# Norm affine parts on GpSimd, the shared expert last, and `dbu` four states at a time, in a Mamba plus mixture-of-experts layer

## What is computed

```python
xn = layernorm(x)
x_proj, z = split(xn @ W_in + b_in)             # 256 + 256 channels
u  = silu(x_proj)
B, C = split(u @ W_xproj + b_xproj)             # 16 states each
dt = softplus(u @ W_dt + b_dt)
h_t = h_(t-1) * exp(dt_t * A) + (dt_t * u_t) * B_t      # per channel and state
y_t = sum over states of h_t * C_t, + D * u_t
x = x + (y * silu(z)) @ W_out + b_out
xn2 = layernorm(x)
scores = softmax(xn2 @ gate_w.T); top 2 of 8 by scores + gate_bias
x = x + sum_e mlp(xn2, w1[e], w2[e], w3[e]) * weight_e + mlp(xn2, sw1, sw2, sw3)
mlp(x, w1, w2, w3) = (silu(x @ w1.T) * (x @ w3.T)) @ w2.T
```

## Time and profile before

| | |
|---|---|
| median of three runs | 1247.91 us |
| the profiled execution's own time | 1250.07 us |
| its span in the trace | 1248.3 us |
| PE busy | 1167.9 us (94%) |
| DVE busy | 1140.5 us (91%) |
| ACT busy | 1140.1 us (91%) |
| POOL (GpSimd) busy | 1043.5 us (84%) |
| DMA, mean | 122 GB/s |

### The profile page before, as it was taken

One profiled execution on the slowest core, in us unless ns is written; L12 is line 12 of the kernel. 1 busy time (PEld: TensorE's weight loads), 2 busy tenths in 40 slices (PEclk: granted clock), 3 DMA queues, 4 the chain that ended last, 5 costly groups with the idle time before them and its releaser, 6 DMA issues.

```text
span 1248.3 us, 24503 instructions
## 1 busy us (share of the span) xinstructions
PE 1167.9 (94%) x7200; PEld 952.1 (76%) x7200; DVE 1140.5 (91%) x1833; ACT 1140.1 (91%) x1980; POOL 1043.5 (84%) x534
## 2 busy tenths in 40 slices
PE   6465699999999999999999999999999999999998
PEld 2244487878888787887878788888878788888887
DVE  0799999999999999999999999999999999999853
ACT  5674989999999999999999999999999999998854
POOL 2998999998998898999889899899889989986500
PEclk8666899999999999999999999999999999999999
DMA  7434150703325060433406042331506133150000
GB/s 265 181 128 153 39 242 9 288 11 146 152 83 207 9 274 23 156 140 136 160 13 275 8 192 104 145 151 62 225 8 250 46 145 143 71 219 1 18 10 9
DMA packets 47955, 152.91 MB, mean 122 GB/s; under 512 B 4512, under 2 KB 29472, under 8 KB 31392
## 3 DMA queue, kind: packets, MB, share of 16 engines
q1 hardware_dynamic: 47904, 152.28, 31.8%
HBM read 147.03 MB, written 5.24 MB: 122 GB/s over the span
## 4 chain that ended last, share of the span: by engine, by line
POOL 44%; PE 23%; issue 18%; ACT 9%; DVE 3%; DMA 1%; POOLq 1%; ACTq 0%; DVEq 0%; SPq 0%
POOL dbu L767 31%; PE h L1034 10%; POOL hc L777 8%; PE mixed L1003 6%; PE y_acc L1016 4%; ACT da L674 2%; POOL w_s L754 2%; POOL dt_s L750 2%; DVE hc L869 1%; ACT mixed L717 1%; ACT silu L710 1%; PE mixed L984 1%; DMA c_all<-bc_rows 1%; ACT L674 1%; PE mixed L977 1%
## 5 line engine op out<-in xcount | busy, mean ns | idle before, releaser
L767 POOL TENSOR_TENSOR dbu<-w_s,b_all 128x1024 f32<-128x1024 f32 x256 | 606.5, 2392 | 1.5 <-DMA c_all<-bc_rows 1.3
L777 POOL TENSOR_TENSOR hc<-hc,c_all 128x1024 f32<-128x1024 f32 x128 | 305.4, 2386 | 109.1 <-DVE hc L869 106.6
L674 ACT ACTIVATE da<-dt_s,a_neg 128x512 f32<-128x512 f32 x512 | 341.9, 687 | 43.2 <-DVE hc L869 24.1
L869 DVE TENSOR_TENSOR_SCAN hc<-da,dbu 128x512 f32<-128x512 f32 x256 | 302.0, 1212 | 26.3 <-ACT da L674 18.6
L869 DVE TENSOR_TENSOR_SCAN da<-da,dbu 128x512 f32<-128x512 f32 x256 | 308.4, 1216 | 14.0 <-POOL dbu L767 12.4
L1016 PE MATMUL y_acc<-ident,hc 128*128 128x128 f32 x2048 | 295.5, 282 | 24.4 <-POOL hc L777 24.3
L1016 PEld LDWEIGHTS y_acc<-ident,hc 128*128 128x128 f32 x2048 | 251.8, 146 | 76.5 <-POOL hc L777 35.8
L1003 PE MATMUL mixed<-w_s,g 128*128 128x128 f32 x2304 | 284.1, 276 | 3.1 <-DVE g L911 2.9
L1003 PEld LDWEIGHTS mixed<-w_s,g 128*128 128x128 f32 x2304 | 272.4, 192 | 18.7 <-issue 9.3
L1034 PE MATMUL h<-x_hi,w_hi 128*128 128x512 f32 x576 | 273.0, 474 | 9.3 <-ACT silu L710 6.3
L1034 PE MATMUL h<-x_hi,w_lo 128*128 128x512 f32 x576 | 228.2, 396 | 0.0
(11 more groups left out here) (79 smaller groups left out, 1047.6 us busy)
## 6 DMA issues: line engine op xcount, KB each, us to landing
b_all<-bc_rows SPq DMA_DIRECT2D x64, 1024.0 KB, 6.9
c_all<-bc_rows SPq DMA_DIRECT2D x64, 1024.0 KB, 9.2
xt<-in_x SPq DMA_DIRECT2D x16, 256.0 KB, 2.8
res<-in_x SPq DMA_DIRECT2D x16, 256.0 KB, 2.8
out<-acc SPq DMA_DIRECT2D x16, 256.0 KB, 3.3
silu<-in_w SPq DMA_DIRECT2D x6, 256.0 KB, 4.5
w_s<-in_w SPq DMA_DIRECT2D x1, 1152.0 KB, 7.8
bc_rows<-bc_rows_s SPq DMA_DIRECT2D x16, 64.0 KB, 1.6
```

The costliest lines, as they stand in the source:

```text
L674: act.activation(da[a % DA_SLOTS][:, :], dt_s[:, c, :], ACT.Exp, scale=a_neg[:, a:a + 1]).then_inc(decay_made, 1)
L767: pool.tensor_tensor(dbu[:, at:at + AT_ONCE, :], w_s[:, c, None, :].broadcast_to([P, AT_ONCE, T]), b_all[:, s:s + AT_ONCE, :], ALU.mult).t ...
L777: pool.tensor_tensor(pair, pair, c_all[:, s:s + 2, :], ALU.mult).then_inc(c_by_pool, 1)
L869: dve.tensor_tensor_scan(dst, ring[:, :], dbu[:, a % DBU_SLOTS, :], 0.0, ALU.mult, ALU.add).then_inc(scanned, 1)
```

## The change

1. `norm1` and `norm2` go from ACT to POOL: `(x - mean) * rstd`, four `tensor_scalar` with the moments and `rstd` as per-partition operands. `nb1` and `nb2` on DVE go away, with their tiles `shift` and `shift2`. `agg1` and `agg2` wait for the norm of the sequence before.
2. The shared expert is the last of the nine. `sc.7` scales the output of the last routed expert in its bank, and a new PE task `shared` adds the shared expert's 16 matmuls into the same bank. One `comb` goes away (8 in place of 9). `shared` waits for `sc.7`.
3. `AT_ONCE` = 4: one `dbu` makes four steps (8 instructions for each sequence in place of 16).
4. `BY_DVE` has 14 steps in place of 16: the products of the steps 28 and 29 go to POOL as one more `hcp`.
5. New order tables on every engine, and no loop: all 16 windows are written out.

```diff
-AT_ONCE = 2
+AT_ONCE = 4
-BY_DVE = [0, 1, 4, 5, 8, 9, 12, 13, 16, 17, 20, 21, 24, 25, 28, 29]
+BY_DVE = [0,1,4,5,8,9,12,13,16,17,20,21,24,25]
...
-        h3.0-1 h3.1-1 red.26 red.27 h3.2-1 red.28 red.29 h1.3-1 eo.0-1 h1.4-1 h1.5-1 red.30 red.31 h1.6-1
...
+        red.30-1 red.31-1 h3.5-2 eo.1-2 h3.6-2 red.0 red.1 h1.7-2 h1.8-2 h1.9-2 gy.1-1 eo.2-2 h3.7-2 red.2
...
-            with eng.Fori(LOOP.start, LOOP.stop) as n:
-                window(n)
-            for n in range(LOOP.stop, END_FROM):
-                window(n)
...
+            for n in range(START_TO + 1, END_FROM):
                 for what, a, off in WINDOW[name]:
...
+                elif what == "norm1":
+                    wait_apart(pool, rstd1_made, m + 1)
+                    for b in range(NB):
+                        last = pool.tensor_scalar(xt[:, b, :], xt[:, b, :], moments[:, b, 0:1], rstd[:, b:b + 1],
+                                                  ALU.subtract, ALU.mult)
+                    last.then_inc(norm1_made, 1)
...
+                    if not first:
+                        wait_apart(dve, read, m)
                     wait_apart(dve, made, m + 1)
...
-                    if what == "comb" and a > 0:
-                        dve.wait_ge(scaled, E * m + a)
+                    if what == "comb" and a == E - 1:
+                        dve.wait_ge(shared_added, m + 1)
+                    elif what == "comb":
+                        dve.wait_ge(scaled, E * m + a + 1)
...
+                elif what == "shared":
+
+                    pe.wait_ge(g_made, UNITS * (m + 1))
+                    pe.wait_ge(scaled, E * (m + 1))
+                    expert_out(mixed_tile("eo", E - 1, m), E, False).then_inc(shared_added, 1)
```

More of the change, by code:

```diff
@@ L72 @@
[L72 to L76, removed]
@@ L83 @@
+        dbu.5+1 norm2.0 hcp.18+1 dbu.6+1 hcp.22+1 dt.0+2 dbu.7+1 w.0+2 hcp.26+1 hcp.28+1 dbu.0+2 hcp.30+1
+        dt.1+2 dbu.1+2
     """,
     "sp": """
-        spread.3 load.0+2 rows.0+1 spread.0+1 spread.1+1 store.0-2 loadres.0 spread.2+1
+        load.0+2 store.0-2 spread.2+1 spread.3+1 loadres.0 rows.0+2 spread.0+2 spread.1+2
     """,
@@ L161 @@
+        rows.0+4 spread.0+4 spread.1+4
     """,
@@ L605, in _, with task @@
             act.wait_ge(const_steps, 2)
-            def task(what, a, m, n, off):
-                first = isinstance(m, int) and m == 0
+            def task(what, a, m):
+                first = m == 0
                 if first and what in ("bcc", "dlc", "skip"):
@@ L620, in task @@
                     act.activation(w13_hi[:, a * W13:(a + 1) * W13], stages[a], ACT.Copy).then_inc(hi_made, 1)
-                elif what == "norm1":
-                    act.wait_ge(shift1_made, m + 1)
-                    for b in range(NB):
-                        last = act.activation(xt[:, b, :], xt[:, b, :], ACT.Identity,
-                                              bias=shift[:, b:b + 1], scale=rstd[:, b:b + 1])
-                    last.then_inc(norm1_made, 1)
                 elif what == "x_tc":
@@ L943, in transposes, with expert_out, task @@
                 return last
-            def task(what, a, m, n, off):
-                first = isinstance(m, int) and m == 0
+            def expert_out(tile, e, begins=True):
+                for b in range(NB):
+                    for f in range(NF):
+                        slot, at = (NF * e + f) % G_SLOTS, (NF * e + f) * DM
+                        last = pe.matmul(as_blocks(tile)[:, b, :], g[:, slot, b * P:(b + 1) * P],
+                                         w2_s[:, at:at + DM], start=(begins and b == 0 and f == 0),
+                                         stop=(b == NB - 1 and f == NF - 1),
+                                         skip_group_check=not begins)
+                return last
+            def task(what, a, m):
+                first = m == 0
                 if what == "warm":
@@ L969, in task @@
                         pe.wait_ge(g_made, UNITS * m + NF * (a + 1))
-                    which, uses = bank_of(what, a, n, off)
+                    which, uses = bank_of(what, a, m)
                     tile = mixed[which]
```

503 lines of the change are left out of this document (228 added, 275 removed).

## The result

The changed kernel takes 1292.67 us (median of four runs, 1291.28 to 1294.23) beside 1248.79 us of the kernel before on the same chip: a ratio of 1.035, 95% interval 1.0329 to 1.0371. It is slower by 44 us. The prediction was 1240.5 us with a range to 1262; it was wrong.

What follows compares the result with a forecast made beforehand. PE (69.5 us a period) and POOL (69.2) were to bound the middle together. From 1250.1: -11.6 middle, +5.5 start, -1.2 end gave 1242.8, or 1240.5 us for the median of runs; range 1229 to 1262.

Steps and rivals of the forecast that it cites:

- I take 0.40: Price in us of one norm piece on POOL, so 3.2 us for the eight in a period.
- from above: Upper bound for a norm piece on POOL: 0.47 us, so 3.8 us for eight.
- a norm piece over 0.6 us (POOL is then over 71 by work alone): Named sign in the profile that the prediction is wrong: POOL's norm pieces too dear.
- I take 70.6 us: Period of one middle sequence, between 69.8 and 73, from 71.57; -11.6 us over 12 periods.
- DVE and ACT have become faster, so scans come earlier: Argument against POOL keeping its 6.2 us of idle time per period, all of it waits for scans.
- so I give the removal of the loop no gain and no loss: Middle: the written-out stretch before the loop showed the same load in 71.57 us, so zero effect.
- PE's floor, 69.5 us: PE's own work in a middle period, without 1.9 us of waits; the change could gain 2 us per sequence at most.
- DVE and ACT.: Busy time per middle period: DVE loses 2.8 us, ACT 3.1 us, both to about 67 us.
- -1.6 for the `dbu` by fours: POOL's work per period: eight fewer `dbu` instructions, each saving 0.20 us of fixed cost, 1.6 us in all.
- I take 42: Start: time in us of the first scan, between 36 unhindered and 46 with a POOL instruction ahead of each `wlo`.
- -1.2 us: End: no `sc` after the last matmuls, `comb.7` follows at once, saving 1.2 us.
- POOL becomes the bound: Rival, chance 0.25: 3.4 us of POOL's scan waits stay per period, period 72.6, time 1264.6 us.

Runs made afterwards that it cites:

- e2: Changed kernel with each four-step `dbu` made as two two-step ones in its place; 1297.61 us, 1.0393 of the kernel before.
- after: The changed kernel as made, with all parts of the change; 1292.67 us, 1.035 of the kernel before.
- e10: Changed kernel with each norm as two broadcast `tensor_tensor` of 512 columns in place of four `tensor_scalar` of 128; 1261.88 us, 1.0096.
- e18: e13 with the epsilon of both norms added on DVE, by four one-column instructions for each norm; 1245.92 us, 0.9977.
- e9: Changed kernel with half of each norm's pieces left out (computation incomplete), nothing put on another engine; 1247.59 us, 0.9988.
- e15: e13 with half of each wide norm left out (blocks 2 and 3 get no affine part); 1233.75 us, 0.9876.
- e4: The kernel before with its hardware loop written out, nothing else changed; 1240.96 us, 0.9943.
- e13: e10 with the expert weights' high halves earlier on ACT and the low halves moved ahead in DVE's queue; 1252.62 us, 1.0026.
- e12: Changed kernel with the nine `wlo` subtractions replaced by one-input multiplications by zero (low halves left out); 1288.85 us, 1.0316.
- e16: e13 with the epsilon of both norms added on DVE, by one four-column instruction for each norm; 1272.85 us, 1.0182.

## Why the prediction was wrong, point by point

These runs keep the order of the new tables in the middle and change what POOL's instructions weigh (e18 has eight small instructions more on DVE). POOL's busy time in one period, and the period:

```
e2     73.6   74.0
after  72.5   73.5
e10    70.3   71.5
e18    69.7   70.8
e9     69.4   70.5
e15    68.6   70.2
```

From `after` to e9 the period is POOL's busy time and 1.0 to 1.2 us. The two ends lie off that line: with `dbu` by twos (e2) it is 0.4 us, and in e15 POOL has 1.6 us to spare.

- **The failed step is one price: "I take 0.40" for a norm piece.** It takes 0.78 from start to start, and even the bound "from above", 0.47, was too low. I built that bound from the line through 512 and 1024 columns of `tensor_tensor`, another operation. The excess on eight pieces is 3.0 us of POOL's work in a period; e9 takes away 3.1 us and gives back 3.05 of the period and 45 us of the time. The text had named the case ("a norm piece over 0.6 us (POOL is then over 71 by work alone)") and left it out of sum and range. The sentence on the Trainium skill (GPSIMD Engine Reference, Elementwise) gave 0.44 and is as far off: the page gives its 1.8 cycles an element as a best case, and has no figure for this operation with two per-partition operands.
- **The price is not all.** With POOL's work as forecast, e9 takes 1247.6 us and not 1240.5. Counted from `dbu.0` to `dbu.0`, as the forecast was, and beside the kernel before, it has +6.2 us in the start, -9.1 in the 12 periods and +0.1 at the end; the forecast had +5.5, -11.6 and -1.2. The changed kernel has +11.0, +26.2 and +5.1.
- **The middle, "I take 70.6 us".** e9 has 69.4 us of work and 70.5, where 69.2 and 70.6 were forecast. That is in part luck: the forecast counted from 71.57 us and gave the loop nothing, while 0.64 us of the way down came from writing it out. With the true price the period is 73.5. POOL's idle time fell to about 1 us of a period, so "DVE and ACT have become faster, so scans come earlier" was right.
- **"so I give the removal of the loop no gain and no loss".** Wrong: e4 gives 7 us. One stretch ahead of the loop showed 71.57 us; but it is the first full sequence with its own idle times (PE busy 70.66 there, 71.11 in the loop), and that difference, 0.45 us, stood in the earlier trace rows. In e4 this stretch still takes 71.58 us, and those behind it 70.93. I read the length of the stretch and not PE's work in it. This error and the price have opposite signs; the change's other parts together cost 52 us against e4.
- **PE's floor, 69.5 us.** The period got no lower than 70.2 (e15). The 1.9 us that I took off were waits of the weight loads, which run beside the matmuls: PE itself was busy 71.11 of 71.57 us in the earlier trace rows, idle for 0.46. In e15 the weight loads still wait 2.0 us of a period, and PE is busy 70.14 of 70.2. So the subtraction gave no floor; what the true one is stays open.
- **DVE and ACT.** 67.65 and 67.99 us where 67 was said: right. The forecast -1.6 for the `dbu` by fours is -1.1 by e2.
- **The start, "I take 42".** The first scan came at 47.0, the end that I had worked out for a `wlo` that waits for one POOL instruction each (46), and not in the middle. e13 shows the place of the `whi` in ACT's queue, and of the `wlo` with them, as the cause. The forecast itself was for `dbu.0` of sequence 2, at 169.7; it starts at 175.2, +11.0 us against +5.5. POOL's waits up to there are 12.6 us, as forecast (12.5). The 5.5 us too few are the eight norm pieces again (3.1), four POOL instructions that take 0.4 to 0.5 us longer each beside the `wlo` (4.95 and 1.71 in place of 4.55 and 1.25, together 1.7), and `dbu.0` of the first sequence, which began at 32.7 and not at 31.3; some smaller terms go the other way.
- **The end, "-1.2 us".** The `sc` behind the last matmul is gone as said, and PE never waits for `sc.7`. But the stretch from sequence 14 on is 6.2 us longer; in e9 it is 1.1. Its first period (sequence 14 to 15) takes 76.6 us in place of 70.8, and still 74.4 in e9 and 74.1 in e15, so most of that isn't POOL's work; in the changed kernel POOL itself waits for a scan there, 3.5 us at 1104.56. No run took that apart.
- **The rival "POOL becomes the bound"** (0.25) was the right case by a different mechanism: I gave it idle time that stays, 1264.6, where it was work, and 1292.7. The range ended at 1262, below even the rival's own point.

The Trainium skill (SBUF — State Buffer, the section on the two sides) was used for two inputs in SBUF. This trace agrees with a wait that lasts a whole instruction: 0.69 us alone, up to 5.0 beside a `dbu` of 4.95. The condition is wider than I had it. The Trainium skill (VectorE: DVE Perf Modes, Mode 2×_2P) says that an instruction with one SBUF source can take both read ports, each for one half of it. e12 (0.41 us alone for 512 columns, where two inputs take 0.67), e16 (four columns wait) and e18 (one column doesn't) agree with it; what divides the four columns was not measured apart.

**What is best.** The fastest complete kernel is e4, the one before with the loop written out, 0.9943 (0.9926 to 0.996); it beats both. The change with its norms in the wide form, the high halves early and the epsilon by columns (e18) is at 0.9977 (0.9966 to 0.9988): 46.8 us under the change as made, and still 5 us over e4. Why it stays above e4, with nearly the same period (70.8 and 70.9), is the start and the end: sequence 2's first scan at 171.0 against 165.7, and 224.3 against 220.2 us from sequence 14 on.

## What to carry to other kernels

Before work is moved to an engine that will be near the bound, its price there must come from a row of the same operation and the same kind of operands; if no row has it, the case "twice as dear" belongs in the range with its full weight, since the doubled price of eight cheap instructions in each of 16 rounds was worth 45 us here. Where every engine runs a list in order, a part of a change cannot be judged by putting it alone into the old lists (68 to 293 us worse), but its weight can be taken away inside the new ones. And look at the form before the place: the same norm as two broadcast instructions gave 31 us, the same addition by single columns 27.

## What the runs showed that I had not expected

- On GpSimd 128 columns with two per-partition operands take 0.80 us (0.78 from start to start, 6.1 ns a column), 512 columns with a full and a broadcast input 1.04 us (2.0 ns), with two full ones 1.28 us.
- A VectorE `tensor_scalar` of four columns and one input, 0.17 us alone, takes 1.32 us in the median beside GpSimd; one of one column is never held up in 128 instances (141 to 156 ns).
- The loop costs 0.64 us of a period of 71.57, seen as longer busy time of PE with the same matmuls.
